# The next block's query products ahead of the transpositions of the finished outputs, in a four-stage transformer kernel

## The reference

```python
x = x + tanh(g_xattn[0]) * cross_attention_0(norm(x), ctx)   # 16 heads of 16, 77 context tokens, mask on queries
x = x + tanh(g_ffn[0])   * mixture(norm(x))                  # 8 experts, top 2, and a shared one
x = x + tanh(g_xattn[1]) * cross_attention_1(norm(x), ctx)   # then a feed-forward of 1024 and two norms
x = x + tanh(g_ffn[1])   * ternary_ffn(norm(x))

# both attentions, the part that the change touches:
q = (norm(x) @ Wq + bq);  k = ctx @ Wk + bk;  v = ctx @ Wv + bv      # split into 16 heads of 16
attn = softmax(q @ k.T / sqrt(16), masked);   out = (attn @ v) @ Wo + bo
```

## Time and profile before

| what | value |
|---|---|
| time, median of 3 runs | 1235.08 us (1235.06 to 1236.01) |
| profiled execution, its own time | 1233.72 us |
| its span | 1232.0 us |
| mean granted clock of TensorE | 0.981 of full speed |
| busy: TensorE / weight loads | 1160.3 us (94%) / 1085.2 us (88%) |
| busy: VectorE / ScalarE / GpSimd | 990.5 us (80%) / 781.3 us (63%) / 676.2 us (55%) |
| one turn of the first attention (161.40 to 175.68 us) | 14.28 us |

### The profile page before, as it was taken

The page is one execution under the profiler, slowest core; times in us unless marked ns, Lnnn a source line. Parts: engine busy times, 40 slices in busy tenths (PEclk is TensorE's granted clock), DMA queues, the critical chain, the costliest instruction groups (busy, mean ns, idle before and its releaser), DMA issues.

```text
span 1232.0 us, 26547 instructions
## 1 busy us (share of the span) xinstructions
PE 1160.3 (94%) x9040; PEld 1085.2 (88%) x9041; DVE 990.5 (80%) x2045; ACT 781.3 (63%) x1489; POOL 676.2 (55%) x772
## 2 busy tenths in 40 slices
PE   6999999989889999999699999998999999899998
PEld 5999999879778999999689999997899998788887
DVE  6899999756897766666689999996987887888887
ACT  4777777668464555555377777775444546777874
POOL 5444333243105556553788777721454656788885
PEclk9999999979999999999899999999999999999999
DMA  4211121113102333333543333313000000000001
GB/s 129 56 53 53 53 57 57 46 61 112 52 1 61 109 106 109 104 105 97 130 74 66 68 67 62 62 30 103 5 2 0 0 0 1 9 18 26 26 26 35
DMA packets 70276, 68.74 MB, mean 56 GB/s; under 512 B 24576, under 2 KB 62208, under 8 KB 69952
## 3 DMA queue, kind: packets, MB, share of 16 engines
q1 hardware_dynamic: 55920, 47.77, 12.8%
q0 software_dynamic: 12576, 18.62, 8.1%
q10 hardware_dynamic: 1712, 1.50, 0.4%
HBM read 44.00 MB, written 18.61 MB: 51 GB/s over the span
## 4 chain that ended last, share of the span: by engine, by line
PE 74%; DVE 11%; ACT 5%; issue 5%; POOL 4%; DMA 1%; ACTq 0%; DVEq 0%; POOLq 0%; SPq 0%
PE PSUM L798 13%; PE PSUM L800 13%; PE PSUM L799 13%; PE PSUM L899 8%; PE PSUM L887 6%; PE PSUM L878 5%; PE PSUM L897 2%; POOL s_t_gh L2659 2%; PE PSUM L810 2%; PE PSUM L851 1%; PE PSUM L908 1%; PE PSUM L1959 1%; ACT s_m_xn L1456 1%; PE PSUM L2848 1%; PE PSUM L2849 1%
## 5 line engine op out<-in xcount | busy, mean ns | idle before, releaser
L2209 POOL TENSOR_TENSOR s_f_h_lo<-s_f_h,s_f_h_hi 128x512 fp32r<-128x512 f32 x64 | 93.4, 1466 | 102.9 <-ACT s_f_h_hi L2153 102.3
L1382 POOL DMA_INDIRECT s_m_tile_x<-normed_x,s_tokens x78 | 96.8, 1241 | 75.1 <-DVE s_tokens L1673 53.7
L899 PEld LDWEIGHTS PSUM<-s_a_v_diagonal,s_a_prob_t 128*128 128x128 f32 x1024 | 125.9, 192 | 0.0
L899 PE MATMUL PSUM<-s_a_v_diagonal,s_a_prob_t 128*128 128x36 f32 x1024 | 125.2, 268 | 0.0
L728 ACT ACTIVATE s_a_prob_t<-PSUM 128x640 f32<-128x640 f32 x128 | 90.0, 703 | 36.6 <-PE PSUM L887 34.9
L474 DVE TENSOR_REDUCE s_a_row_max<-PSUM 128x8 f32<-128x640 f32 x128 | 104.7, 818 | 7.3 <-PE PSUM L878 4.0
L481 DVE TENSOR_TENSOR s_a_less<-PSUM,s_a_row_max 128x640 f32<-128x640 f32 x128 | 104.9, 820 | 4.4
L1049 POOL DMA_INDIRECT s_x<-sorted_y,s_slots x60 | 95.3, 1588 | 19.7 <-issue 13.6
L2147 ACT ACTIVATE s_f_h<-PSUM,s_cols 128x512 f32<-128x512 f32 x64 | 44.0, 688 | 89.6 <-PE PSUM L800 89.0
L887 PE MATMUL PSUM<-s_ident,s_a_prob 128*128 128x128 f32 x640 | 93.7, 277 | 1.0
L798 PE MATMUL PSUM<-s_m_x_hi,s_m_up_w 128*128 128x256 f32 x312 | 91.8, 294 | 1.1 <-issue 1.0
(11 more groups left out here) (327 smaller groups left out, 4222.5 us busy)
## 6 DMA issues: line engine op xcount, KB each, us to landing
sorted_y<-s_m_tile_y SPq DMA_DIRECT2D x39, 256.0 KB
s_a_kd<-s_a_k_parts SPq DMA_DIRECT2D x126, 40.0 KB
s_x<-x SPq DMA_DIRECT2D x16, 256.0 KB, 3.1
s_a_ctx<-ctx SPq DMA_DIRECT2D x32, 128.0 KB, 2.8
s_moe_raw<-moe_w SPq DMA_DIRECT2D x16, 256.0 KB
normed_x<-s_m_xn SPq DMA_DIRECT2D x16, 256.0 KB, 3.1
y<-s_x SPq DMA_DIRECT2D x16, 256.0 KB, 2.1
s_late_raw<-moe_w SPq DMA_DIRECT2D x11, 256.0 KB, 2.9
```

Of the source, the lines that this page charges most:

```text
L899: last = pe.matmul(a.o_ps[:, 2 * c:2 * c + 2, :], a.prob_t[j % 2][:, c, :], v[:, j // BT, 0, 2 * c:2 * c + 2], start=False, stop=c == PC - ...
L1382: pool.indirect_dma_start(m.tile_x[n % 2][:, t, :], None, d["normed_x"], bass.IndirectOffsetOnAxis(ap=tokens[:, BT * n + t:BT * n + t + 1] ...
L2209: pool.tensor_tensor(f.h_lo[m % 4][:], f.h[m % 4][:], f.h_hi[m % 4][:].bitcast(F32), ALU.subtract).then_inc(f.h_split, 1)
```

## The change

In TensorE's `body` of an attention turn the two steps behind the scores of unit 3 change places. The other engines' streams, all waits and all signals are the same.

```diff
--- before.py
+++ after.py
@@ -988,10 +988,10 @@
                 transpose_prob(b, 0)
                 score(b, 2)
                 score(b, 3)
+                if ahead:
+                    queries(b.next())
                 if behind:
                     transpose_o(b.last(), 0)
-                if ahead:
-                    queries(b.next())
                 transpose_prob(b, 1)
                 weigh_values(b, 0)
                 transpose_prob(b, 2)
```

## The result

The time went from 1235.08 us to 1268.83 us (median of 5 runs, 1267.29 to 1270.49; before in the same comparison 1234.63 to 1236.01). The ratio is 1.0262, 95% interval 1.0233 to 1.0291: slower by 33.7 us. 1268.7 was predicted.

A forecast was written before the change was run, and what follows sets the result against it. TensorE was taken to bound the kernel, busy 14.24 of 14.28 us per turn. A 1.40 us delay less 0.19 slack gives 1.21 per turn; 28 x 1.2 = 33.6 us on 1235.08 gives 1268.7, range 1256 to 1281.

The forecast's parts named there:

- The forward move of the products gains nothing: TensorE: query products start 0.41 us earlier, nobody waits for them; 0 gained, at most the 0.19 us pause per turn.
- The outputs' transpositions end 1.40 us later: TensorE: placed behind the 12 query products, the four transpositions end 1.40 us later, bounds 1.34 to 1.49.
- ScalarE takes 0.19 off as slack: ScalarE: slack ahead of unit 2's exponential, behind the outputs' rounding, absorbs 0.19 us on average, bounds 0.09 to 0.26.
- Unit 2's transpositions carry the rest through: TensorE: they wait for ScalarE's read-out of unit 1, so the shift of 1.21 us per turn passes whole.
- The path over bank 6 would alone cost about 1.0: VectorE's later outputs' residue holds up unit 0's weighted values, sharing bank 6; about 1.0 us per turn even without ScalarE's path.
- the second wait of 0.2 to 0.3 us: TensorE would stand still 0.2 to 0.3 us ahead of unit 2's transpositions, besides about 1.0 ahead of unit 0's weighted values.
- Nothing in the rest of the turn gives it back: All three engines' streams stand 1.21 us later in the same relation, so the next turn starts 1.21 us later.
- rival B: ScalarE's 3.4 us without work per turn takes up half the delay: 17 us slower, 1252 us; chance 0.05.
- 28 turns: Turns with a block behind and a block ahead change, in both attentions together; 28 x 1.2 = 33.6 us.
- A, the clock falls: TensorE's new pauses bring 3.4 us at half speed into every second turn: 24 us more, 1293 us; chance 0.05.
- C: One alternation less on TensorE, and slack for the outputs' rounding: 7.5 us gained, 1227.5 us; chance 0.015.
- D: The outputs' rounding has enough slack and nothing is gained: no change in time, 1235 us; chance 0.015.

The follow-up runs named there:

- with ScalarE's path shortened: Changed kernel, with ScalarE's exponential of unit 2 put ahead of the outputs' rounding: turn 15.37 us, time 1276.74 us, ratio 1.0333 to the kernel before.
- with TensorE's order of before: Kernel before, with only ScalarE's stream changed, the exponential of unit 2 ahead of the outputs' rounding: turn 15.34 us, time 1269.68 us, ratio 1.0282.
- three, six and twelve matmuls: Number of the twelve query matmuls put ahead of the outputs' transpositions, against the kernel before: three 1242.04 us, six 1251.03, twelve (the change itself) 1268.83.
- The kernel before with the short residue: Kernel before, with VectorE's residue of the outputs left out but for 32 columns: time 1236.56 us, ratio 1.0013.

## Why the prediction was right, step by step

- *The forward move of the products gains nothing.* Right. The pause of 0.19 us behind the scores stayed: the weight loads of the first product start at 181.66 and the row names 0.19 us of issue ahead of them. The reason given, that nobody waits for the products, was too strong: it holds for bringing them forward, but they had only 0.06 us of slack to the other side.
- *The outputs' transpositions end 1.40 us later* (1.34 to 1.49). Measured 1.48 when the two turns are laid on one another at the scores of unit 2 (167.82 before, 180.59 after): 183.21 + 0.60 = 183.81 against 169.56 + 12.77 = 182.33; the mean of twelve turns is 1.47. The first product took 0.24 in place of the 0.117 assumed, although it follows scores and not transpositions, so the alternation saved nothing. This term was mis-sized by 0.07.
- *ScalarE takes 0.19 off as slack.* Measured 0.26 as the delay less the turn's cost, 0.23 of it in the start of the exponential. Mis-sized by 0.07 too, within the bounds given (0.09 to 0.26).
- *Unit 2's transpositions carry the rest through.* Right: 1.47 - 0.26 = 1.21. That the sum came out at 1.21 to the hundredth is luck, as the two errors of 0.07 cancel; the mechanism is not.
- *The path over bank 6 would alone cost about 1.0.* Measured 15.37 - 14.28 = 1.09 with ScalarE's path shortened, and 1.06 with TensorE's order of before. In the changed kernel the two tie within about 0.1 us, where I had ScalarE's ahead by 0.2; the second wait of 0.2 to 0.3 us that I expected ahead of unit 2's transpositions did not appear.
- *Nothing in the rest of the turn gives it back* (rival B). Right: what the delay has above the slack stands in the turn in full, at three, six and twelve matmuls.
- *28 turns.* 28 x 1.21 = 33.9 us, the medians differ by 33.75. The profiled spans differ by 36.7, though, 3 us more than the turns. One place is the second turn of the second attention, where the step from one block's token transpositions to the next's is 18.67 us (before 14.88) and the clock is at half speed in it:

```profile
647.90:654.70 6.80, 6.80 (x34) 6.80 (x32) 5.17 (x11) 3.34 (x7) 6.27 (x6) 0.51 0.33 58
```

This is not the change's pause at work: the first of this attention's 14 new waits for the residue ends at 660.73, behind the stretch, and the last of the first attention's 14 ended at 247.1. What stands ahead of the stretch are pauses of 0.80 and 0.77 us, ahead of 645.48 and 647.59, and the kernel before has the same two, ahead of 627.51 and 629.61, with the clock at full speed behind them. The kernel before with the short residue has a stretch at half clock near there too (633.7 to 637.1). So stretches at half clock vary near the starts of the attentions, and a part of the time varies with them. That median and prediction agree to 0.1 us is luck to this extent; the profiled execution of the change, 1270.49, is 1.66 above its own median.
- *A, the clock falls.* It did not in the change's turns (1.00 from 30 to 240 us and from 660 to 862 us).
- *C and D* (a gain, or nothing) needed a slack of 1.4 us; it is 0.26.

## What to carry to other kernels

When an order of steps on a full engine is changed, price the step that moves back by who waits for it, and follow that waiter's whole queue: here 1.5 us of delay hit a queue with 0.26 us of slack, and the three steps queued behind the rounding carried the delay back to the engine that had given the place away. A step that no row names as awaited may still have no slack, if its waiter was busy until just then; subtract the end of the one from the start of the other before calling it free. And where two paths rejoin within a tenth of a microsecond, shortening either one alone shows almost nothing (here 0.01 and 0.12 us of 1.21): only both together (0.63) show that the loss is in them.

## What the runs showed of the hardware

The granted clock stood at full speed through 210 us of turns in which TensorE paused for 0.96 us in each 15.5, and fell to half speed in two turns of three where it paused for 1.50 in every turn. Behind the same two pauses of 0.80 and 0.77 us in the second attention it fell in the changed kernel's profile and not in the one before. The first product behind scores took 0.24 us and the first behind transpositions 0.20, against 0.117 for the others: here the first product costs about 0.1 us more behind either kind. VectorE's residue of the outputs took 0.69 us (691 to 693 ns) whenever it had waited for its input, and mostly 0.66 when it followed other work (656 to 661 ns in 25 of 29 in the kernel before).
